# Clip of the experts' linear half on GpSimd, the MLP's input normalisation on ScalarE, and the bias sum behind the clips

## The reference, cut to what matters

```python
h2 = _layernorm(x1, ln2_g, ln2_b)
mlp = jax.nn.gelu(h2 @ W1 + b1, approximate=False) @ W2 + b2
...
g = jnp.minimum(p1[..., 0::2], LIMIT)
lin = jnp.clip(p1[..., 1::2], -LIMIT, LIMIT)
act = g * jax.nn.sigmoid(ALPHA * g) * (lin + 1.0)
```

## Time and profile before

| what | value |
|---|---|
| median of three runs | 1107.53 us |
| the profiled execution: its time | 1108.31 us |
| the profiled execution: its span | 1106.5 us |
| TensorE busy | 1005.9 us, 91% |
| VectorE busy | 858.5 us, 78% |
| ScalarE busy | 671.2 us, 61% |
| GpSimd busy | 558.8 us, 51% |
| chain that ended last, by engine | PE 53%, DVE 23%, POOL 10% |
| mean granted clock of TensorE | 0.983 |

### The profile page before, as it was taken

The page is one execution under the profiler, slowest core; times in us unless marked ns, Lnnn a source line. Parts: engine busy times, 40 slices in busy tenths (PEclk is TensorE's granted clock), DMA queues, the critical chain, the costliest instruction groups (busy, mean ns, idle before and its releaser), DMA issues.

```text
span 1106.5 us, 21501 instructions
## 1 busy us (share of the span) xinstructions
PE 1005.9 (91%) x7672; PEld 607.0 (55%) x7672; DVE 858.5 (78%) x2054; ACT 671.2 (61%) x998; POOL 558.8 (51%) x783
## 2 busy tenths in 40 slices
PE   3679999999999999999999999999999999999987
PEld 2234656556465565646556474655646565564635
DVE  7668887878888787898878878887888878787616
ACT  3126665657566575756657576565766666575775
POOL 6516364553736355283535537454463645535263
PEclk8689999999999999999999999999999999999999
DMA  5730514215051330605124051511405142140000
GB/s 113 171 77 1 130 35 99 65 43 102 20 118 46 85 80 7 138 21 118 46 72 85 8 135 30 114 50 58 88 20 129 35 102 62 47 89 20 19 20 10
DMA packets 86396, 74.93 MB, mean 68 GB/s; under 512 B 9426, under 2 KB 80019, under 8 KB 86291
## 3 DMA queue, kind: packets, MB, share of 16 engines
q1 hardware_dynamic: 84210, 72.78, 28.0%
q10 hardware_dynamic: 2080, 0.79, 0.3%
HBM read 36.33 MB, written 30.15 MB: 60 GB/s over the span
## 4 chain that ended last, share of the span: by engine, by line
PE 53%; DVE 23%; POOL 10%; issue 9%; ACT 2%; DMA 2%; SPq 0%; DVEq 0%; POOLq 0%; ACTq 0%
DVE mx L1017 9%; PE ps L516 8%; PE ps L498 7%; POOL h L1225 6%; PE ps L501 5%; PE ps L695 5%; PE ps L656 5%; PE ps L482 5%; PE ps L635 4%; PE ps L533 3%; PE ps L528 2%; DVE xn L874 2%; DVE junk L882 2%; POOL r L1168 2%; PE ps L550 1%
## 5 line engine op out<-in xcount | busy, mean ns | idle before, releaser
L1017 DVE TENSOR_REDUCE mx<-ps 128x2 f32<-128x512 f32 (+1 forms) x512 | 307.0, 616 | 48.9 <-PE ps L501 46.3
L772 ACT ACTIVATE pt<-ps 128x1024 f32<-128x1024 f32 (+1 forms) x256 | 232.9, 917 | 148.4 <-PE ps L482 146.5
L1178 POOL TENSOR_SCALAR_AFFINE_SELECT pt<-pt 128x512 f32<-128x512 f32 x256 | 169.3, 662 | 271.9 <-ACT pt L772 271.9
L498 PE MATMUL ps<-kd,qz 128*128 128x256 bf16 (+1 forms) x1024 | 186.4, 265 | 30.4 <-DVE mx L1017 24.6
L501 PE MATMUL ps<-mask,identb 128*128 128x512 bf16 (+1 forms) x512 | 181.8, 357 | 0.0
L498 PEld LDWEIGHTS ps<-kd,qz 128*128 128x128 bf16 x1024 | 74.3, 98 | 184.2 <-DVE mx L1017 92.2
L635 PEld LDWEIGHTS ps<-m,act_t 128*128 128x128 f32 x1024 | 127.9, 191 | 48.9 <-DVE act_t L1104 31.3
L635 PE MATMUL ps<-m,act_t 128*128 128x128 f32 x1024 | 142.1, 282 | 9.3 <-DVE act_t L1104 9.3
L516 PE MATMUL ps<-pt,va 128*32 128x256 f32 (+1 forms) x2048 | 146.2, 364 | 3.5 <-ACT ot L777 2.0
L482 PE MATMUL ps<-qz,kd 128*128 128x512 bf16 (+1 forms) x512 | 139.9, 355 | 2.2 <-DMA qz<-minus_maxima 1.2
L818 ACT ACTIVATE lin<-ps,mbias 128x512 f32<-128x512 f32 x128 | 87.8, 686 | 74.3 <-PE ps L630 40.6
(11 more groups left out here) (154 smaller groups left out, 1578.6 us busy)
## 6 DMA issues: line engine op xcount, KB each, us to landing
qz<-qk_parts SPq DMA_DIRECT2D x32, 384.0 KB
kd<-qk_parts SPq DMA_DIRECT2D x32, 384.0 KB
qk_parts<-qp SPq DMA_DIRECT2D x16, 384.0 KB, 2.4
qk_parts<-kp SPq DMA_DIRECT2D x16, 384.0 KB, 2.6
xl<-L_attn_x SPq DMA_DIRECT2D x16, 256.0 KB, 3.1
qk_parts<-qp SPq DMA_DIRECT2D x16, 256.0 KB, 2.7
qk_parts<-kp SPq DMA_DIRECT2D x16, 256.0 KB, 2.9
xnr<-xn SPq DMA_DIRECT2D x16, 256.0 KB, 2.7
```

The costliest lines, as they stand in the source:

```text
L498: nc.tensor.matmul(o[:, par, lo:], qz[q][:, p, par, P * i:P * (i + 1)], kd[q][:, p, P * (i - 1) + lo:P * (i + 1)], start=par == 0, stop=False,
L772: nc.scalar.activation(pt[:, n % NPT, :, 0:w_q], src, ACT.Exp, scale=SCALE).then_inc(exp_ok.sem, 1)
L1017: nc.vector.tensor_reduce(mx[:, i, h:h + 2], src, AX.X, ALU.max).then_inc(mx_ok.sem, 1)
L1178: sel1 = nc.gpsimd.affine_select(out=pt[:, s, :, 0:P], in_=pt[:, s, :, 0:P], compare_op=ALU.is_ge, fill=0.0, base=0, pattern=[[0, HG], [1, ...
```

## The change

The clip moves from VectorE's program to GpSimd's: clip(0) and clip(1) stand ahead of GpSimd's wait for the mean and variance of x1, clip(2) to clip(7) behind the inverse root, and the bias sum x1b behind them. GpSimd no longer normalises x1. It computes the negated mean (nmu) and its product with r3 (m3), and ScalarE forms h2 as r3 * x1 + m3, in four activations (Identity with a scale and a bias for each token) behind ga of expert 4 (H2_AT = 4).

```diff
--- before.py
+++ after.py
@@ -53,6 +53,7 @@
 NEG = -1e30
 TIE = -1e-37
 CONSTS = 4
+H2_AT = 4
 
 
 class Signal:
@@ -174,6 +175,8 @@
         mv2 = sb("mv2", [P, NT, 2])
         r3t = sb("r3t", [P, NT])
         r3 = sb("r3", [P, NT])
+        nmu = sb("nmu", [P, NT])
+        m3 = sb("m3", [P, NT])
         h2 = sb("h2", [P, NT, D])
         h2T = sb("h2T", [P, T])
         hid = sb("hid", [P, NJ, T])
@@ -257,8 +260,8 @@
         x1b_ok = signal("x1b_ok", 1)
         st2_ok = signal("st2_ok", 1)
         mv2_ok = signal("mv2_ok", 1)
-        r3_step = signal("r3_step", 2)
-        h2_ok = signal("h2_ok", 1)
+        r3_step = signal("r3_step", 4)
+        h2_ok = signal("h2_ok", NT)
         h2T_ps = signal("h2T_ps", 1)
         h2T_ok = signal("h2T_ok", 1)
         w1_ps = signal("w1_ps", NJ)
@@ -819,6 +822,12 @@
                         nc.scalar.activation(ga[:, e % 2], bank(3 * (e % 2)), ACT.Gelu_apprx_sigmoid, bias=mbias[:, e, 0:1]).then_inc(ga_ok.sem, 1)
                         if nx2 and e == 3:
                             nfn_in()
+                        if e == H2_AT:
+                            act.wait_ge(*done(r3_step, b))
+                            act.wait_ge(*done(x1_ok, b))
+                            act.wait_ge(*done(h2T_ps, b - 1))
+                            for t in range(NT):
+                                nc.scalar.activation(h2[:, t], x1[:, t], ACT.Identity, bias=m3[:, t:t + 1], scale=r3[:, t:t + 1]).then_inc(h2_ok.sem, 1)
                         if e == 6:
                             act.wait_ge(*done(h2T_ps, b))
                             act.wait_ge(*done(w1_ps, b - 1))
@@ -1070,11 +1079,6 @@
                     dve.wait_ge(*done(gth_ok, b + 1))
                     nc.vector.tensor_tensor(gpre[:], bank_t(5), rows["bg"][:].unsqueeze(1).to_broadcast([P, NT, D]), ALU.add).then_inc(gpre_ok.sem, 1)
                 if main:
-                    def clip(e):
-
-                        dve.wait_ge(*done(lin_ok, b, e + 1))
-                        nc.vector.tensor_scalar(lin[:, e % 2], lin[:, e % 2], 1.0 - LIMIT, 1.0 + LIMIT, ALU.max, ALU.min).then_inc(clip_ok.sem, 1)
-
                     def gate(e):
 
                         dve.wait_ge(*done(ga_ok, b, e + 1))
@@ -1083,7 +1087,6 @@
                         nc.vector.scalar_tensor_tensor(out=gc[:, e % 2], in0=ga[:, e % 2], scalar=G_LIMIT, in1=bank(3 * (e % 2) + 2),
                                                        op0=ALU.min, op1=ALU.mult).then_inc(gc_ok.sem, 1)
 
-                    clip(0)
                     for e in range(E):
                         gate(e)
                         if e == 0:
@@ -1102,8 +1105,6 @@
                         dve.wait_ge(*(done(down_ps, b, e - 2) if e >= 3 else done(down_ps, b - 1)))
                         dve.wait_ge(*done(clip_ok, b, e + 1))
                         nc.vector.tensor_tensor(act_t[:, e % 3], lin[:, e % 2], gc[:, e % 2], ALU.mult).then_inc(act_ok.sem, 1)
-                        if e < E - 1:
-                            clip(e + 1)
                         if e == 0:
                             dve.wait_ge(*done(t1_ok, b))
                             dve.wait_ge(*done(s1_ok, b))
@@ -1216,14 +1217,21 @@
                         pool.wait_ge(*done(qkmid_ok, b + 2, n + 1))
                         nc.gpsimd.tensor_tensor(parts[:, 2], rest[:], parts[:, 1], ALU.subtract).then_inc(qklo_ok.sem, 1)
                 if main:
+                    def clip(e):
+
+                        pool.wait_ge(*done(lin_ok, b, e + 1))
+                        nc.gpsimd.tensor_scalar(lin[:, e % 2], lin[:, e % 2], 1.0 - LIMIT, 1.0 + LIMIT, ALU.max, ALU.min).then_inc(clip_ok.sem, 1)
+
+                    clip(0)
+                    clip(1)
                     pool.wait_ge(*done(mv2_ok, b))
                     inv_root(r3[:], r3t[:], mv2[:, :, 1], 1.0, r3_step, b, 0, ((h2_ok, b - 1, None),))
-                    pool.wait_ge(*done(r3_step, b))
-                    pool.wait_ge(*done(h2T_ps, b - 1))
-                    apart(pool, b)
-                    for t in range(NT):
-                        ts = nc.gpsimd.tensor_scalar(h2[:, t], x1[:, t], mv2[:, t, 0:1], r3[:, t:t + 1], ALU.subtract, ALU.mult)
-                    ts.then_inc(h2_ok.sem, 1)
+                    nc.gpsimd.tensor_scalar(nmu[:], mv2[:, :, 0], -1.0, 0.0, ALU.mult, ALU.add).then_inc(r3_step.sem, 1)
+                    pool.wait_ge(*done(r3_step, b, 3))
+                    nc.gpsimd.tensor_tensor(m3[:], nmu[:], r3[:], ALU.mult).then_inc(r3_step.sem, 1)
+                    for e in range(2, E):
+                        clip(e)
+                    pool.wait_ge(*done(x1_ok, b))
                     pool.wait_ge(*done(s_ok, b - 1))
                     nc.gpsimd.tensor_tensor(x1b[:], x1[:], rows["b2"][:].unsqueeze(1).to_broadcast([P, NT, D]), ALU.add).then_inc(x1b_ok.sem, 1)
```

## The result

The changed kernel takes 1192.51 us (median of four, 1192.23 to 1195.27) against 1107.57 us before (median of four): ratio 1.0772, 95% interval 1.0753 to 1.079. It is slower by 85 us, 5.3 us a batch. The direction was forecast; the forecast of 1122 us with a range up to 1132 was wrong.

What follows compares the result with a forecast made beforehand. Bound: TensorE, its MLP start set by waits, GpSimd's normalisation on the path. MLP 0.92 us later a batch, times 16 is 14.7 us; 1108.31 + 14.7 = 1123.0, in the median's terms 1122.2 us; range 1111 to 1132.

Steps and rivals of the forecast that it cites:

- Bound and tail: TensorE busy 8.80 of 8.80 us in the MLP tail, which can only be shifted; the MLP's start decides.
- Part 1: VectorE loses eight clip steps of about 0.34 us; clip(1) and clip(2) gone bring the moments 0.66 us earlier.
- Part 2: Clips on GpSimd take 0.62 us each, bounds 0.42 and 1.16 us.
- Part 3: Clip(2) queues behind GpSimd's inverse root and small products; at product of expert 2, 0.66 us gain becomes 1.30 us loss.
- Part 4: Normalisation on ScalarE: removes 4.54 us of GpSimd operations, adds four activations of 0.38 us, 1.52 us in all.
- The rule: Trainium skill: two-input VectorE and SBUF-reading GpSimd instructions block each other, the second waiting for the whole first; products would wait.
- rival 2: VectorE's products held up by GpSimd's clips, 0.54 and 0.55 us: 2.0 us a batch, 32 us, 1140; chance 0.07.
- The clock: Sign against the forecast: TensorE's granted clock falls in its longer wait, which no earlier row shows; no size given.
- three signs: Prediction wrong if product(2) starts within 8.6 us of up(0), products exceed 0.8 us, or the granted clock falls.

Runs made afterwards that it cites:

- experiment 2: Changed kernel with GpSimd's (max, min) clips replaced by the cheap operation (mult 1, add 0), clip itself left out: 1151.66 us, ratio 1.0395.
- experiment 4: Clip(2) moved ahead of GpSimd's wait for the moments: 1107.35 us with the cheap operation (mult, add), 1145.8 us in the changed kernel with real clips.
- experiment 1: Kernel before plus 21 single GpSimd operations behind its last store: (max, min) on 128x512 1.91 to 1.93 us, (mult, add) 0.62 us.
- experiment 3: TensorE's waits filled with unread matmuls: seven added to experiment 2's kernel, 1141.7 us; fifteen added to the changed kernel, 1187.35 us.

## Why the prediction was wrong

**Bound and tail: right.** The tail stayed as long as it was, and the window ahead of it grew by 5.17 us on average, 83 of the 85 us over 16 batches.

**Part 1: right in its place, too large.** The moments were to come 0.66 us earlier; they came 0.39 earlier with the cheap operation (7.17 us after the first up projection, against 7.56) and 0.07 later in the changed kernel, because the product of expert 0 took 0.96 and 1.10 us for 0.68 and, in the changed kernel, waited 0.24 us for its clip as well.

**Part 2: the step that failed.** "The nearest row is its tensor_scalar with immediates of the same shape": I took 0.62 us by shape and kind of operand, and the pair of arithmetic operations decides: 1.91 us. The upper bound of 1.16 us, from a two-input operation, was no bound either. The price stood in the trace. In the earlier trace rows GpSimd's normalisation takes 0.79 us at best for 128 columns, where (mult, add) takes 0.62 for 512. I read its spread as GpSimd being held up by VectorE and never asked why even its minimum was so high. Clips at 1.91 us are worth 1187.35 - 1141.70 = 45.7 us, both with filled waits. Yet this step alone doesn't account for the miss: even with clips of 0.62 us and the waits filled the kernel takes 1141.7 us, outside the range that ended at 1132.

**Part 3: right.** Root, small products and the start of clip(2) came within 0.1 us of the chain, and at the higher clock the order alone is worth 34 us with cheap clips and 42 with real ones. It is the forecast's core, and moving one line confirmed it.

**Part 4: right in size, 1.64 us with the last activation's end, steps of 0.38 us.** Moved alone it gives no gain: 1106.66 at best.

**The rule and rival 2: the second step that failed.** The forecast's chain put the held product at nothing, and I gave the rival 0.07, judging by products beside tiles of 128 columns; the clips have 512. It happened. At the same 0.62 us and with filled waits the kernel took 1141.7 us, not 1122, and rival 2 had said 1140. Its parts are other than I chained them, though: three products are held by 0.3 to 0.4 us, not two by 0.55. Of the 1.06 us that the MLP starts late in most batches (17.64 for 16.58), 0.25 are the late product 2 (product 0 was held), 0.31 product 2 itself and 0.37 product 5, all read from the trace; the rest I have not placed.

How long a product is held follows from one figure. In the changed kernel and in experiment 2, 103 products started up to 0.2 us behind a clip. All but one, with which it was the clip that was held, ended 1.15 to 1.16 us after that clip's start, whether the clip took 1.91 us or 0.62. So the clip was in the way for its first 0.47 us (1.16 less the 0.69 of a free product) in both. Real clips in the order of experiment 4 show the other side, a product that starts 1.02 us into a clip of 1.92 (at 527.21) and isn't held:

```profile
528.22 0.67 DVE L1107 TENSOR_TENSOR act_t<-lin,gc 128x512 f32<-128x512 f32 x1
```

The bias sum holds a product until 1.13 us after its own start, of 1.28. On the Trainium skill's rule (SBUF — State Buffer, "Who interferes with whom"), whoever comes second waits for the whole of the first: the trace agrees, but for the last 0.15 us, for the bias sum (a product of 1.78 us that starts 0.06 us behind a sum of 1.28), not for the clips, whose 1.91 us held a product by 0.42 to 0.46 only.

**The clock** I had named as a risk without a price. It cost 5 to 6 us here and 10 in experiment 2. Two of the three signs that I had named against the forecast came true, products over 0.8 us and a clock that falls in the longer wait; the third, product 2 within 8.6 us, did not.

| step from | to | us | shown by |
|---|---|---|---|
| before, 1107.6 | forecast, 1122.2 | 14.6 | chained from rows, not run by itself |
| forecast | cheap operation, waits filled, 1141.7 | 19.5 | products held beside clips: 0.93 us a batch read from the trace, the rest not placed |
| that | changed kernel, waits filled, 1187.4 | 45.7 | clips of 1.91 us (experiment 1, and the two kernels of experiment 3 against each other) |
| that | changed kernel, 1192.5 | 5.2 | lower clock behind the wait (experiment 3; 6.5 by the two ratios) |

## What to carry to other kernels

Price an operation that moves to another engine by a row with the same arithmetic on that engine, and look at time per column: two rows of different width give it. Before moving work into an engine's queue, list what it now stands behind; here one line's place was worth 47 us. Look at what a moved operation will run beside: these clips, though they filled idle time of GpSimd, lengthened VectorE's products by 0.3 to 0.46 us wherever one started just behind a clip.

## What the runs showed of the hardware

- GpSimd's tensor_scalar goes by its pair of operations. With immediates on 128x512 fp32, alone, (mult, add) and (mult, mult) take 0.62 us; (max, min), (max, mult), (mult, min) and (subtract, mult) take 1.92 to 1.93; max alone takes 1.49. Each was measured once.
- A GpSimd clip of 128x512 holds up a VectorE product of two SBUF operands during its first 0.47 us only, whether it takes 0.62 us or 1.91 (102 held products). It seems to be in the way while it reads. That it is the reading is inferred; no run shows it directly.
- Between starts 0.01 us apart or less either can be the one held: in experiment 1 it was GpSimd's (2.48 us for 1.93, the product 0.69), at 555.24 in the changed kernel VectorE's product (1.15). A GpSimd operation that starts 0.05 us or more behind a product's start is the one held: in experiment 1 it got under way 0.55 us after the product's start.
- Added matmuls made a kernel 10 us faster, by keeping TensorE's granted clock at 1.00 where it had averaged 0.80 over 8.7 us of most batches.
